# Attention scores of two heads at once on the two halves of TensorE's rows, in an attention, memory and mixture-of-experts layer

## The chip, the cores and the metric

The kernel runs on 1 core of one Trainium2 chip. The metric is the device time of one execution in microseconds (us). An execution is one launch that takes all inputs from the chip's main memory and leaves the output there.

## The reference, cut to what matters

The layer has an attention part and a part with 8 experts, each with a residual and a layer norm behind it. x has 8 batches of 512 positions and 256 features; there are 16 heads of 16 features. In the attention part a memory runs beside the softmax (decaying sums of outer products of 6-vectors), whose score gates a second value.

```python
B, T, D = x.shape                      # 8, 512, 256
H = decay_logits.shape[0]; dh = D // H # 16 heads of 16
qkv = (x @ qkv_w.T + qkv_b).reshape(B, T, 3, H, dh)
scores = jnp.einsum('bhtd,bhsd->bhts', q, k) * dh ** -0.5
scores = jnp.where(causal, -jnp.inf, scores)
attn = jax.nn.softmax(scores, axis=-1)
seq_out = jnp.einsum('bhts,bhsd->bhtd', attn, v)
...                                    # memory: lines, norms, decayed cumulative sums, gated
return (seq_out + gated * mem_val) @ out_w.T + out_b
# then: x = layernorm(x + attention); top-2 of 10 gates, 8 experts of 256 x 256; x = layernorm(x + ffn)
```

## The kernel before, in words

The program has three parts. The opening (about 0 to 95 us) computes the memory's projections of all batches, folds two weight matrices into one, and projects batch 0. The middle (about 78 to 545 us) is the attention of batch 0 to 7, with the memory's elementwise work on POOL beside it. Phase 3 (to the end) is the output projection, the layer norms and the experts; its weights are loaded and split beside the last batch.

The middle is made of groups: 4 heads of one batch, so 4 groups a batch, 32 in all. A group has 12 units (`UNITS`). Units 0 to 3 are the four heads' first tile of the triangle (512 columns), 4 to 7 the second (384), 8 and 9 the third (256, two heads each), 10 and 11 the last (128, padded to 256, two heads each). Scores are needed twice. `pe_max_scores` computes them with queries on the partitions, and DVE takes each row's maximum with the causal mask (`dve_max`, line 468, written to nmax); this runs 8 units (`LEAD`) ahead. `pe_exp_scores` computes them again with keys on the partitions, less the maximum, and ACT takes the exponential (`act_exp`, line 411) into Pr. POOL zeroes the upper triangle of the diagonal tiles (`pool_mask`, line 612). `pe_values` (line 338) multiplies Pr with V, in four strips of 17 of the array's columns, one strip a head, during the following group.

Numbers that must be more exact than one pass of the array gives are split in a high and a rest part. For that, Q and K stand in SBUF as stacks: three parts of 16 rows (high, high, rest against high, rest, high), 48 rows of zeros up to row 96 (`STACK`), and in rows 96 and 97 minus one in K against the high and rest part of the row maximum in Q. So a score matmul uses 96 or 98 of the array's 128 rows, and holds one head.

Each group also carries two of the 8 projections of the next batch (`pe_project`, line 374, six matmuls, at units 4 and 10), into one PSUM bank, J_ps. For j = 0 to 3 (Q and K) ACT copies the high part to HL (`act_project`, line 419), DVE the rest (`dve_project`, line 477), and SP writes HL to the main memory (`sp_projected`, line 623), from where `sp_stack` reads the stacks of a group in six DMAs. There is one HL, so the copy of j + 1 waits until the write of j has landed. For j = 4 to 7 ACT copies MV (line 422) and DVE adds to Vn (line 481). The input x of the next batch is split in xhi (ACT, line 438) and xlo (DVE, line 510) at unit 0 of the batch before, ahead of the first projection.

At unit 4 the maxima of the next group are transposed on TensorE (`pe_turn_max`, line 358), copied by DVE in a high and a rest part (`dve_turned_max`, lines 490 and 492), and written by SP with two DMAs to rows 96 and 97 of Q (`sp_max_rows`, line 643); the next group's first exponentials wait for them. At unit 7 ACT copies the values' bank O_ps to Osb (`act_out`), at unit 10 TensorE transposes it (`pe_turn_out`, line 351), and DVE divides by the sums (`dve_normalise`, lines 500 and 503). Both transposes use one bank, ps[5].

The order of all this is written out by hand: `pe_batch`, `act_batch`, `dve_batch`, `sp_batch` list for each engine what it does at which unit, and every engine works through its list in order. `need` waits for a semaphore. DVE's list also holds 36 scans of the memory (line 516), at units 6, 8, 10 or 0, 2, 4 of two groups in three from batch 2 on; POOL's list holds the masks between the memory's steps (lines 801 to 854). PSUM's 8 banks: three for the maxima's scores (S_ps), two for the exponentials' (ST_ps), one each for O_ps, the transposes, and J_ps.

## Time and profile before

| | us |
|---|---|
| median of 3 runs | 828.99 |
| lowest and highest run | 825.13, 829.65 |
| the profiled execution | 834.11 |
| its span, first to last instruction | 832.4 |
| TensorE busy in it | 734.4 (88%) |
| VectorE busy in it | 603.8 (73%) |
| ScalarE busy in it | 351.0 (42%) |
| GpSimd busy in it | 422.3 (51%) |

Engines are named as in the profile: PE is TensorE's matmuls, PEld its weight loads, DVE is VectorE, ACT ScalarE, POOL GpSimd, SP SyncE, which only issues DMAs here. Matmuls are pipelined and their ends are modelled, so PE's busy time holds more than its work; the distance from the start of one matmul to the start of the next is what it really takes in a dense stretch. PEclk is the clock that TensorE was granted, 1.00 being 2.4 GHz and 0.50 being 1.2 GHz. "Idle before, releaser" names what ended a wait.

### The profile page before, as it was taken

The page shows a single profiled execution, that of the slowest core. Times are in us where ns is not written, and L with a number is a line of the kernel's source. Part 1 is how long each engine was busy: PE and PEld are TensorE (multiplying, and loading weights), DVE is VectorE, ACT ScalarE, POOL GpSimd, SP SyncE. Part 2 cuts the span into 40 slices and gives each one's busy share as a digit, 9 for nine tenths or more (in the row PEclk, how much of TensorE's full clock was granted, in tenths as well). Part 3 has the DMA queues.
Part 4 walks back from the last instruction along what each step waited for, and adds up shares of the span by engine and source line. Part 5 has one row for each costly group of instructions (what it writes and reads, how often), then busy time and mean ns, then how long its engine had stood idle before and what let it go on. Part 6 is the DMA issues. An engine that isn't in the chain of part 4 may idle for free.

```text
span 832.4 us, 12395 instructions
## 1 busy us (share of the span) xinstructions
PE 734.4 (88%) x4004; PEld 495.0 (59%) x4004; DVE 603.8 (73%) x2105; ACT 351.0 (42%) x701; POOL 422.3 (51%) x334
## 2 busy tenths in 40 slices
PE   6993998898898998999898998878899899998995
PEld 3452655565565666565565664446677676776774
DVE  2344776778878888889688877736777877787785
ACT  2211555446454545555455555842242242232410
POOL 9200894996665676668476893424134042240410
PEclk9995999999998999999899997899999999999998
DMA  7899589675564574655734747220220302303000
GB/s 274 257 234 165 127 142 144 163 115 104 130 102 84 133 119 100 152 85 138 139 69 105 139 87 170 73 101 2 77 85 18 101 10 93 102 1 102 26 24 27
DMA packets 60420, 89.88 MB, mean 108 GB/s; under 512 B 8234, under 2 KB 37316, under 8 KB 60356
## 3 DMA queue, kind: packets, MB, share of 16 engines
q1 hardware_dynamic: 60356, 89.09, 47.7%
q8 instruction: 32, 0.52, 0.3%
q14 instruction: 32, 0.26, 0.1%
HBM read 54.72 MB, written 33.82 MB: 106 GB/s over the span
## 4 chain that ended last, share of the span: by engine, by line
PE 47%; DVE 23%; DMA 10%; POOL 9%; ACT 4%; issue 4%; SPq 2%; ACTq 0%; POOLq 0%; DVEq 0%
PE ps L1256 15%; PE ps L374 8%; PE ps L338 7%; PE ps L327 6%; PE ps L315 6%; DVE ps L468 5%; DMA Wm<-mem_scratch 3%; DVE Ob L516 3%; DMA Q<-MT 3%; DVE A L1390 3%; ACT X L1242 2%; PE ps L1221 2%; PE ps L232 1%; POOL Pr L612 1%; DVE Z L1276 1%
## 5 line engine op out<-in xcount | busy, mean ns | idle before, releaser
L468 DVE CUSTOM_DVE_ANT_0 ps<-ps,mask 128x256 f32<-128x256 f32 (+3 forms) x512 | 236.9, 509 | 31.8 <-PE ps L315 31.0
L411 ACT ACTIVATE Pr<-ps 128x512 f32<-128x512 f32 (+2 forms) x384 | 190.1, 528 | 114.8 <-PE ps L327 110.6
L327 PE MATMUL ps<-Q,K 98*128 98x256 f32 (+2 forms) x512 | 173.2, 380 | 28.9 <-DMA Q<-MT 21.9
L315 PE MATMUL ps<-K,Q 96*128 96x256 f32 (+2 forms) x512 | 157.9, 355 | 23.2 <-DVE nmax L468 22.5
L1256 PE MATMUL ps<-ew_hi,XT 128*128 128x512 f32 x512 | 176.2, 403 | 0.0
L1390 DVE SCALAR_TENSOR_TENSOR A<-ps,cw,A 128x256 f32<-128x256 f32 x256 | 123.6, 483 | 48.5 <-PE ps L1256 36.0
L327 PEld LDWEIGHTS ps<-Q,K 98*128 98x128 f32 x512 | 94.1, 197 | 104.8 <-ACT Pr L411 61.0
L612 POOL TENSOR_SCALAR_AFFINE_SELECT Pr<-Pr 128x512 f32<-128x512 f32 x128 | 88.3, 704 | 103.2 <-ACT Pr L411 100.8
L315 PEld LDWEIGHTS ps<-K,Q 96*128 96x128 f32 x512 | 103.0, 203 | 45.8 <-DVE nmax L468 28.3
L1256 PEld LDWEIGHTS ps<-ew_hi,XT 128*128 128x128 f32 x512 | 97.0, 189 | 21.2 <-issue 0.3
L1256 PE MATMUL ps<-ew_rest,XT 128*128 128x512 f32 x256 | 101.2, 395 | 0.0
L338 PE MATMUL ps<-Pr,V 128*17 128x512 f32 (+3 forms) x1024 | 99.9, 465 | 0.8 <-POOL Pr L612 0.8
L1194 POOL TENSOR_TENSOR A<-A,X 128x512 f32<-128x512 f32 x16 | 20.6, 1286 | 148.1 <-ACT A L1248 148.1
L468 DVE DVE_READ_ACCUMULATOR2_ANT nmax<- 128x1 f32 x512 | 69.5, 136 | 0.0
L419 ACT ACTIVATE HL<-ps,qkb 128x512 fp32r<-128x512 f32 x32 | 22.0, 687 | 81.9 <-PE ps L374 57.5
L1256 PEld LDWEIGHTS ps<-ew_rest,XT 128*128 128x128 f32 x256 | 48.6, 190 | 8.6
L374 PE MATMUL ps<-xhi,wqk 128*128 128x512 f32 x128 | 46.8, 450 | 3.5 <-DVE xlo L510 1.9
L852 POOL TENSOR_TENSOR Ob<-Ob,Rl 128x1533 f32<-128x1533 f32 x12 | 34.8, 2903 | 27.6 <-DVE Ob L516 27.6
L801 POOL TENSOR_TENSOR Ob<-Wm 128x511 f32<-128x511 f32 (+1 forms) x12 | 14.2, 1186 | 67.7 <-DMA Wm<-mem_scratch 67.5
L516 DVE TENSOR_TENSOR_SCAN Ob<-sc,Ob 128x512 f32<-128x512 f32 x36 | 45.7, 1269 | 0.0
L854 POOL TENSOR_TENSOR Wm<-Wm,Ob 128x1533 f32<-128x1533 f32 x12 | 43.4, 3613 | 0.9
L374 PE MATMUL ps<-wvc,xhi 128*128 128x512 f32 x128 | 42.8, 415 | 0.4 <-DVE bc L945 0.4
(190 smaller groups left out, 1049.2 us busy)
## 6 DMA issues: line engine op xcount, KB each, us to landing
qk_scratch<-HL SPq DMA_DIRECT2D x32, 512.0 KB, 3.2
Q<-qk_scratch SPq DMA_DIRECT2D x96, 128.0 KB, 4.4
K<-qk_scratch SPq DMA_DIRECT2D x96, 128.0 KB, 5.7
Pr<-xT SPq DMA_DIRECT2D x8, 512.0 KB, 7.0
xraw<-xT SPq DMA_DIRECT2D x8, 512.0 KB, 6.4
mem_scratch<-Rl SPq DMA_DIRECT2D x16, 256.0 KB, 7.5
mv_scratch<-MV SPq DMA_DIRECT2D x32, 128.0 KB, 1.8
Wm<-mem_scratch SPq DMA_DIRECT2D x16, 256.0 KB, 9.3
```

What stands on the lines that cost most here:

```text
L315: last = nc.tensor.matmul(o, Q[0:STACK, hh, P * i:P * i + P], K[0:STACK, hh, 0:n], start=True, stop=True)
L327: last = nc.tensor.matmul(o, K[0:STACK + 2, hh, P * kt:P * kt + P], Q[0:STACK + 2, hh, T - n:T], start=True, stop=True)
L338: last = nc.tensor.matmul(O_ps[32 * h:32 * h + VW, P * kt:T], V[:, kt, GROUP * g + h, :], probs(g % 2, kt, h, 1)[:, 0, :], start=(kt == 0) ...
L374: last = nc.tensor.matmul(J_ps[:], lhs, rhs, start=first, stop=(j < 4 and k == KT - 1 and a == 1))
L411: nc.scalar.activation(probs(g % 2, kt, heads[0], len(heads)), src, ACT.Exp, scale=SCALE).then_inc(s_exp, 1)
L468: last = nc.vector.tensor_tensor_reduce(out=scores, in0=scores, in1=mask[:, T - w:T], scale=1.0, scalar=NEG, op0=ALU.add, op1=ALU.max, acc ...
L516: nc.vector.tensor_tensor_scan(Ob[:, j % 3, :], col(SC_D).to_broadcast([P, T]), Ob[:, j % 3, :], 0.0, ALU.mult, ALU.add).then_inc(s_scan, 1)
L612: nc.gpsimd.affine_select(out=diagonal, in_=diagonal, compare_op=ALU.is_ge, fill=0.0, base=0, pattern=[[0, GROUP], [1, P]], channel_multip ...
L852: step(nc.gpsimd.tensor_tensor(Ob[:, :, 0:T - 1], Ob[:, :, 0:T - 1], Rl[:, i:i + 1, 1:T].to_broadcast([P, 3, T - 1]), ALU.mult))
L854: step(nc.gpsimd.tensor_tensor(Wm[:, lo:lo + 3, 0:T - 1], Wm[:, lo:lo + 3, 0:T - 1], Ob[:, :, 0:T - 1], ALU.add))
L1256: last = nc.tensor.matmul(o, lhs(c, k), rhs(d, k), start=first, stop=(k == KT - 1 and c == 1))
L1390: ins = nc.vector.scalar_tensor_tensor(acc, F_ps[v % 4][:, D * c:D * c + D], cw[:, par, i, e:e + 1], acc, ALU.mult, ALU.add)
```

## The change

- **Stacks.** `STACK` is 48: the three parts without zeros. Heads with an even number in the group have their stack in rows 0 to 47 (maxima in 48 and 49), odd ones in rows 64 to 111 (112 and 113), `HALF` being 64. Q and K are half as long (H // 2), and POOL's memsets of them at the start are two of 32 rows instead of three.
- **Scores in pairs.** `pe_max_scores` and `pe_exp_scores` are called for units u and u + 1 together and issue one matmul for a lower and one for an upper half, into two banks. S_ps has four banks, ST_ps two; the exponentials' pair waits until both have been read. Units 8 and 9, 10 and 11 hold heads 0 and 2, 1 and 3.
- **Banks.** The transposed output goes back to O_ps, the transposed maxima to J_ps, with waits for both.
- **HL, xhi and xlo twice.** HL alternates with j; its parts are written to memory by a DMA each, when each is ready. x is split a batch earlier, at units 10 and 11 of the last group.
- **Order.** Projections on PE at units 0 and 8 (was 4 and 10), their copies on ACT at 1 and 9 (4 and 10) and on DVE at 3 and 11 (5 and 11). The transposed output at unit 8 ahead of the projection (10, behind it), its division at 9 (10). The maxima are still transposed at unit 4, with no projection ahead of them; DVE copies them at 5 (4).
- **DMAs.** Eight for a group's stacks (six), four for the maxima's rows (two), two for HL (one).

```diff
-STACK = 96
+STACK = 48
+HALF = 64
-        S_ps, ST_ps = ps[0:2] + ps[7:8], ps[2:4]
-        O_ps, OT_ps, J_ps = ps[4:7]
-        M_ps = OT_ps
+        S_ps, ST_ps = [ps[0], ps[1], ps[7], ps[5]], ps[2:4]
+        O_ps, J_ps = ps[4], ps[6]
+        OT_ps, M_ps = O_ps, J_ps
...
+        def stacked(t, hh, n):
+            return t[HALF * (hh % 2):HALF * (hh % 2) + n, hh // 2, :]
...
         def pe_exp_scores(pe, b, g, u):
-            need(pe, s_exp, PU, b, UNITS * g + u - 1)
-            for c, h in enumerate(heads):
-                hh = GROUP * g + h
-                o = ST_ps[u % 2][:, c * 256:c * 256 + n]
-                last = nc.tensor.matmul(o, K[0:STACK + 2, hh, P * kt:P * kt + P], Q[0:STACK + 2, hh, T - n:T],
-                                        start=True, stop=True)
-            last.then_inc(s_st, 1)
+            need(pe, s_exp, PU, b, UNITS * g + u)
+            for c in range(len(unit_parts(u)[1])):
+                for v in (u, u + 1):
+                    kt, heads = unit_parts(v)
+                    hh = GROUP * g + heads[c]
+                    n = max(T - P * kt, 2 * P)
+                    ins = nc.tensor.matmul(ST_ps[v % 2][:, c * 256:c * 256 + n],
+                                           stacked(K, hh, STACK + 2)[:, P * kt:P * kt + P],
+                                           stacked(Q, hh, STACK + 2)[:, T - n:T], start=True, stop=True)
+                    if c == len(heads) - 1:
+                        ins.then_inc(s_st, 1)
...
         def pe_turn_out(pe, b, g):
             need(pe, s_oc, NG, b, g + 1)
-            need(pe, s_on, NG, b, g)
...
-        def pe_turn_max(pe, b, g):
+        def pe_turn_max(pe, b, g, projected):
             need(pe, s_max, PU, b, UNITS * (g + 1))
             need(pe, s_mt, 2 * NG, b, 2 * g)
-            need(pe, s_on, NG, b, g - 2)
+            pe.wait_ge(s_lo, projected)
...
-                for u in range(UNITS):
+                for u in range(0, UNITS, 2):
                     pe_exp_scores(pe, b, g, u)
...
-                    if u in (0, 2, 4, 6) and not (first and g == 0):
+                    if u < 8 and not (first and g == 0):
                         pe_values(pe, pb, pg, u // 2)
-                    if u in (4, 10) and not last:
-                        pe_project(pe, b + 1, 2 * g + u // 10)
+                    if u == 8 and not (first and g == 0):
+                        pe_turn_out(pe, pb, pg)
+                    if u in (0, 8) and not last:
+                        pe_project(pe, b + 1, 2 * g + u // 8, NG * b + g + 1 + u // 8)
                     if u == UNITS - LEAD and not (last and g == NG - 1):
-                        pe_turn_max(pe, b + (g + 1) // NG, (g + 1) % NG)
-                    if u == 10 and not (first and g == 0):
-                        pe_turn_out(pe, pb, pg)
+                        pe_turn_max(pe, b + (g + 1) // NG, (g + 1) % NG, min(8 * (b + 1) + 2 * g + 1, 8 * NB))
...
-                    if g == 0 and u == 0 and not last:
-                        act_split_x(act, b + 1)
-                    if u in (4, 10) and not last:
-                        act_project(act, b + 1, 2 * g + u // 10)
+                    if u in (1, 9) and not last:
+                        act_project(act, b + 1, 2 * g + u // 9)
+                    if (g, u) == (NG - 1, 10) and b < NB - 2:
+                        act_split_x(act, b + 2)
...
-                    if g == 0 and u == 0 and not last:
-                        dve_split_x(dve, b + 1)
-                    if u in (5, 11) and not last:
+                    if u in (3, 11) and not last:
                         dve_project(dve, b + 1, 2 * g + u // 11)
-                    if u == UNITS - LEAD and not (last and g == NG - 1):
+                    if u == UNITS - LEAD + 1 and not (last and g == NG - 1):
                         dve_turned_max(dve, b + (g + 1) // NG, (g + 1) % NG)
-                    if u == 10 and not (first and g == 0):
+                    if u == 9 and not (first and g == 0):
                         dve_normalise(dve, pb, pg)
...
             for r in range(2):
-                sp.dma_start(Q[STACK + r:STACK + r + 1, GROUP * g:GROUP * g + GROUP, :].rearrange(
-                    "o h (i t) -> o (h i) t", i=QT).bitcast(F32), MT[:, g % 2, r, :].bitcast(F32)).then_inc(s_mrow[g], 16)
+                for a in range(2):
+                    row = HALF * a + STACK + r
+                    sp.dma_start(Q[row:row + 1, 2 * g:2 * g + 2, :].rearrange("o c (i t) -> o (c i) t", i=QT).bitcast(F32),
+                                 MT[2 * QT * a:2 * QT * a + 2 * QT, g % 2, r, :].bitcast(F32)).then_inc(s_mrow[g], 16)
```

## Rows read from the trace of the kernel before

**Rows 1.** The page: busy us (share of the span) xinstructions.
```profile
PE 734.4 (88%) x4004; PEld 495.0 (59%) x4004; DVE 603.8 (73%) x2105; ACT 351.0 (42%) x701; POOL 422.3 (51%) x334
```

**Rows 2.** Stretches: us, busy per engine, PEclk, DMA share, GB/s.
```profile
130.00:187.40 57.40, 51.35 (x306) 32.58 (x306) 39.84 (x157) 27.28 (x55) 44.66 (x38) 0.94 0.78 140
187.40:486.70 299.30, 273.48 (x1642) 174.58 (x1641) 245.98 (x866) 154.28 (x311) 199.57 (x127) 0.95 0.57 114
486.70:545.00 58.30, 51.46 (x320) 30.45 (x318) 42.39 (x149) 37.46 (x76) 30.15 (x26) 0.85 0.39 102
473.70:486.70 13.00, 12.70 (x85) 8.41 (x85) 9.50 (x42) 7.00 (x16) 11.33 (x7) 1.00 0.77 107
```

**Rows 3.** Timeline of PE, one group: start, us, line, out<-in, columns, count.
```profile
477.30 0.63 PE L374 MATMUL ps<-wvc,xhi 128*128 128x512 f32 x2
...
478.69 0.28 PE L378 MATMUL ps<-bc,pick 96*128 96x256 f32 x1
...
479.17 0.48 PE L327 MATMUL ps<-Q,K 98*128 98x256 f32 x2
479.48 0.34 PE L315 MATMUL ps<-K,Q 96*128 96x384 f32 x1
479.66 0.40 PE L327 MATMUL ps<-Q,K 98*128 98x512 f32 x1
...
480.22 1.05 PE L338 MATMUL ps<-Pr,V 128*17 128x512 f32 x8
...
481.54 0.41 PE L315 MATMUL ps<-K,Q 96*128 96x256 f32 x2
481.78 0.40 PE L327 MATMUL ps<-Q,K 98*128 98x512 f32 x1
482.02 0.40 PE L315 MATMUL ps<-K,Q 96*128 96x256 f32 x2
482.35 0.84 PE L338 MATMUL ps<-Pr,V 128*17 128x384 f32 x8
483.11 0.50 PE L327 MATMUL ps<-Q,K 98*128 98x512 f32 x1
```

**Rows 4.** Waits from 95 to 545 us: total us, times, longest.
```profile
DVE MT L490 <- PE ps L358: 37.6, 26, 3.2
...
DVE rec L500 <- PE ps L351: 27.2, 22, 2.4
...
ACT HL L419 <- DMA qk_scratch<-HL: 16.2, 5, 4.1
...
POOL Ob L801 <- DMA Wm<-mem_scratch: 8.8, 1, 8.8
```

**Rows 5.** Timelines of DVE and PE at a batch's head, and stretches there.
```profile
258.71 2.63 DVE L510 TENSOR_TENSOR xlo<-xraw,xhi 128x1024 fp32r<-128x1024 f32 x1
...
262.27 0.77 PE L315 MATMUL ps<-K,Q 96*128 96x512 f32 x1 [2.31 <-DVE nmax L468]
...
259.00:263.00 4.00, 1.69 (x13) 0.94 (x13) 4.00 (x13) 0.98 (x2) 3.92 (x2) 0.80 0.95 107
263.00:266.00 3.00, 3.00 (x14) 1.78 (x14) 0.87 (x4) 0.00 (x0) 2.26 (x2) 0.50 0.36 142
```

**Rows 6.** Timeline of ACT: two exponentials and the wait before them.
```profile
483.65 0.98 ACT L411 ACTIVATE Pr<-ps 128x512 f32<-128x512 f32 x2 [0.83 <-PE ps L327]
...
481.74 1.09 ACT L411 ACTIVATE Pr<-ps 128x512 f32<-128x512 f32 x2 [0.99 <-PE ps L327]
```

**Rows 7.** SP's issue of the maxima's rows, and all their landings (line 643).
```profile
487.36 1.14 SPq L643 DMA_DIRECT2D Q<-MT  x2
...
DMA to landing us min/median/max: 1.8/2.7/11.4
```

**Rows 8.** The chain in the opening: start, us, what.
```profile
15.72 2.62 DMA qk_scratch<-HL
...
18.43 0.69 ACT HL L419
19.15 0.76 DVE HL L477
19.93 2.62 DMA qk_scratch<-HL
```

156 lines of the change are left out of this document (88 added, 68 removed).

## The prediction

> **What bounds the kernel now.** I read the page's busy times first, then one row per stretch for the middle of the kernel, then one undisturbed group on TensorE matmul by matmul, then the waits. The profiled execution took 834.11 us, 832.4 of it span. TensorE (PE) has the largest share, VectorE (DVE) the next [rows 1]. The middle of the kernel repeats one unit of work, a "group" (4 heads of one batch). From 187.4 to 486.7 us there are 20 of them, so 299.3 / 20 = 14.97 us each, in which DVE is busy 246.0 / 20 = 12.3 and POOL 10.0; an undisturbed group takes 13.0 with PE busy 12.7 [rows 2]. So PE sets the pace of the good groups, DVE stands close behind, and 2 us a group are lost on top.
>
> PE's 13.0 us in an undisturbed group, from where each matmul starts [rows 3]: a 512-column score matmul holds PE 0.24 us (481.78 to 482.02), a 384 one 0.18, a 256 one 0.12. A group has 16 scores for the maxima and 16 for the exponentials, each 4 x 0.24 + 4 x 0.18 + 8 x 0.12 = 2.6, together 5.2. Two projections are 2 x 1.39 (477.30 to 478.69), bias and transposes 0.48 and 0.2. The values (L338) take 1.05 and 0.84 us for 512 and 384 columns. That is 0.21 per 128 columns for all 8 matmuls of a call; a score streams 128 columns in 0.06 (0.24 / 4), so eight in turn would take 0.48 or more. The strips of 17 columns do run side by side. They stream 0.86 + 0.65 + 0.43 + 0.22 = 2.15. Round them stands a toll: the last score before them is over at 482.02 + 0.24 = 482.26, they start at 482.35, stream until 483.00, and the next score matmul loads at 483.11 and runs 0.1 later. So it costs 0.1 to go into another shape of the array and 0.2 to come out, 1.2 in four blocks. Sum: 5.2 + 2.8 + 0.7 + 2.15 + 1.2 = 12.05, so about 1 us of the 13.0 is waiting.
>
> The lost 2 us: ACT waits for the write of HL to land (16.2 us in five waits), DVE waits for the transposed maxima (37.6) and for the transposed output (27.2) [rows 4]. The worst place is at the head of a batch: the split of x on DVE takes 2.63 us, PE waits 2.31 for maxima behind it, the granted clock falls from full (2.4 GHz) to half (1.2 GHz), and the next matmuls take twice as long [rows 5].
>
> **The change part by part.**
> *Scores in pairs.* If the two halves run side by side as the column strips do, 16 pairs cost what 16 single ones cost: 2.6 instead of 5.2, so -2.6 us a group. The trace has no row halves; the bounds are 0 (they don't overlap) and -2.6. Between them: the strips of the values load only 17 columns of weights, the pairs 128 each, and a transpose, as short as the load allows, takes 0.11 to 0.12. Were two loads to follow each other, each of 16 pairs would cost at least 0.22, in all 3.5: -1.7. I take -2.6, nearest to the only rows with several tiles at once.
> The Trainium skill, "TensorEngine Tiling (Array Packing)", Key Properties, says that different tiles can load weights and multiply in parallel; it backs the value taken. The same section says that changing the tiling mode drains the engine, which speaks against this change; the trace agrees (0.1 in, 0.2 out).
> *Changes of shape.* Scores are now a third shape. The extra changes are projection to scores at unit 0, the transposed maxima at unit 4, and in and out of the full array at unit 8: four more, 0.2 each, +0.8. PE's own work is then 12.05 - 2.6 + 0.8 = 10.3.
> *Both ST banks at once.* A pair of exponentials' scores now waits until both banks are read. Turn-round: 0.4 for the matmuls, then two reads on ACT at 0.98 to 1.09 [rows 6], 1.4 to 1.5 us. Units 0, 4 and 8 give PE more own work than that between two pairs; at 2 and 6 it is about even; after unit 10 it is not: the projection's copy (0.4 to 0.7) and two reads stand before PE's next pair, against 0.4 of own work. I put 1.0 to 1.6 of waiting a group, so 11.3 to 11.9 for the loop of PE and ACT.
> *The maxima's rows.* DVE copies them at its unit 5, 7.3 us after the group's start in this order of work. SP then issues four DMAs instead of two, at 0.57 each (1.14 for two), and one lands after 1.8 to 2.7: 7.3 + 1.7 + 1.8 to 2.7 = 10.8 to 11.7 [rows 7]. This chain is as long as the loop: whenever DVE is late, the next group is late by as much. Behind them on SP's queue is only the next projection's write.
> *DVE.* Nothing is taken from it: 12.3 us a group remain from 187.4 on, more than PE and ACT want. It is the new bound. The waits for the transposes go, since PE now issues them before a projection and not behind it, and DVE reads a unit later. The split moves to the end of a batch with a second x: the same DVE time, but no projection waits for it. The second HL takes away the five waits for its landing. Eight stack DMAs for six add 0.9 us to SP, which is idle at that point; HL's write in two parts starts earlier.
> DVE's work is uneven (three scans of 1.2 us in two groups of three), so I don't expect 12.3 but about 1.1 more for meeting PE and ACT, as much as PE pays now in its best groups: 13.4. Saving: 20 x (14.97 - 13.4) = 31 us. With no loss it would be 53.
> *Before 187.4.* The first projections follow each other every 4.2 us because HL must land (2.6) first [rows 8]; without that, PE 1.6, ACT 0.7 and DVE 0.76 make 3.1. Three times 1.1 is 3 us; it can be lost again in the full DMA queues behind (0 to 5). The shorter memset on POOL hides behind these. Then POOL sets the pace: it is busy 44.7 of 57.4 us in 130 to 187.4 [rows 2] and waits 8.8 for its rows [rows 4], with masks between its long steps. I give this stretch 5 us (1 to 9).
> *The last batch and after.* No projections, the scores of the exponentials alone in pairs, clock 0.85 [rows 2]: 2 us (-1 to 4). Phase 3 is untouched: 0.
> Sum: 31 + 3 + 5 + 2 = 41. 834.1 - 41 = 793.1 for a profiled execution. Those of before have a median of 828.99, 5.1 lower: 788.
>
> **The rivals.**
> A. The weights of the two halves load one after the other, or the row chain or ACT's handshake costs a microsecond more than above. PE then stands at 11.2 plus waits, or the groups at 14.2. For it: 128 columns of weights each, and a chain with no slack. Against: the strips. 20 x 0.8 = 16 less is saved: 804.
> B. The halves don't overlap at all (both write PSUM at once, or nothing makes them tiles). PE's own work is 12.05 + 0.8 = 12.9, with ACT's wait 14.2 and DVE's unevenness about 15.0, as now. What is left is 3 + 5 and some of the landing waits: 824. Against: the strips of the values do overlap.
> C. Slower: the clock. PE's own work falls from 12.05 of 14.97 (80%) to 10.3 of 13.4 (77%), and its waiting gathers at the group's end (1 us, with DVE late 3). The trace shows the fall after a wait of 2.31 us, 3 us at half speed and more [rows 5]. A microsecond at half speed costs 0.5 x 0.77 = 0.39. The 41 us are gone when each of 28 groups spends 41 / 28 / 0.39 = 3.8 us more at half speed: a granted clock of about 0.80 in the middle instead of 0.95 [rows 2]. With one such fall of 5.5 us in each group: 788 + 28 x 5.5 x 0.39 = 848. Against: falls today follow waits of over 2 us, and the change removes the two commonest.
>
> **How the numbers follow.** Forecast 0.57, A 0.24, B 0.07, C 0.12. The forecast's ends: 20 x (14.97 - 12.3) + 5 + 9 + 4 = 71 saved gives 758; 14.0 a group and nothing elsewhere gives 810. The range runs from 758 to 832, over A and B and into the mild end of C; about 0.05 lies below and 0.12 above. A measurement here tells about 0.5% (4 us) from no change. B lies on both sides of that line and C's mildest cases are within it: faster 0.82, same 0.06, slower 0.12.
>
> **What would show it.** Right: the two scores of a pair start within some 10 ns; the 32 scores of a group take PE under 3 us; no wait of ACT for HL's landing in the middle; DVE's waits for the two transposes are small; the middle has 13 to 14 us a group with DVE busy over 90%. Wrong: starts of a pair 0.11 apart (A) or a whole matmul apart (B); a granted clock under 0.85 from 187 us on (C); PE waiting for the maxima's rows in most groups (A's row chain).

## The result and the profile after

| | before | after |
|---|---|---|
| median, us (4 runs each) | 829.32 | 854.99 |
| lowest and highest | 825.13, 831.29 | 849.70, 855.83 |
| span of the profiled execution | 832.4 | 853.6 |
| mean granted clock in it | 0.946 | 0.891 |

The ratio is 1.0303, 95% interval 1.0245 to 1.0361: 3% slower, where 788 us, 5% faster, had been predicted, and outside the range of 758 to 832. It was measured beside new runs of the kernel before. Here and below a ratio is formed from undisturbed executions alone, so it is not exactly the quotient of the medians beside it.

The page of the changed kernel first: busy times (they answer rows 1), the granted clock in 40 slices, and the two groups of score matmuls.

```profile
span 853.6 us, 12579 instructions
...
PE 690.4 (81%) x4004; PEld 425.8 (50%) x4004; DVE 602.5 (71%) x2105; ACT 349.0 (41%) x701; POOL 409.1 (48%) x333
...
PEclk9996888989696899898797798587999999999998
...
L490 DVE CUSTOM_DVE_ANT_0 ps<-ps,mask 128x256 f32<-128x256 f32 (+3 forms) x512 | 237.7, 512 | 118.9 <-PE ps L331 118.7
...
L346 PE MATMUL ps<-Q,K 50*128 50x256 f32 (+2 forms) x512 | 102.2, 437 | 91.6 <-DMA Q<-MT 50.5
...
L331 PE MATMUL ps<-K,Q 48*128 48x256 f32 (+2 forms) x512 | 81.1, 356 | 11.1 <-DVE nmax L490 8.7
```

The same two kinds of line on the page of the kernel before:

```profile
PEclk9995999999998999999899997899999999999998
...
L327 PE MATMUL ps<-Q,K 98*128 98x256 f32 (+2 forms) x512 | 173.2, 380 | 28.9 <-DMA Q<-MT 21.9
```

TensorE is busy 690 us instead of 734 and yet the kernel is longer. The scores of the exponentials (L346, was L327) took 173 us and take 102, but idle time in front of them is 92 us, mostly for the maxima's rows (Q<-MT). The slices of the clock tell of a second thing: behind the opening seven slices stand at 5 to 7 tenths, where the kernel before has one.

The stretches of rows 2, by the same limits:

```profile
core 0: us, PE busy (x) PEld busy (x) DVE busy (x) ACT busy (x) POOL busy (x), PEclk, DMA share, GB/s
130.00:187.40 57.40, 41.85 (x291) 22.60 (x284) 39.05 (x150) 27.42 (x57) 42.42 (x35) 0.85 0.68 143
187.40:486.70 299.30, 236.53 (x1572) 125.18 (x1573) 237.98 (x835) 146.66 (x297) 194.54 (x126) 0.86 0.41 111
486.70:545.00 58.30, 44.21 (x318) 21.79 (x318) 41.31 (x173) 32.82 (x68) 30.18 (x24) 0.82 0.47 134
```

In the middle PE is busy 236.5 us of 299.3 (273.5 before), DVE 238.0 (246.0), at a clock of 0.86 (0.95). No engine is busier than 80%: DVE, which was to be the new bound, has become idler.

The pair itself does what was hoped. The timeline of TensorE, against rows 3:

```profile
start us, us, engine line op out<-in xcount [idle before <-releaser]
305.60 0.28 PE L374 MATMUL ps<-ident,nmax 128*16 128x128 f32 x1
305.83 0.44 PE L346 MATMUL ps<-Q,K 50*128 50x384 f32 x2
306.11 0.39 PE L331 MATMUL ps<-K,Q 48*128 48x512 f32 x2
306.43 0.41 PE L359 MATMUL ps<-Pr,V 128*17 128x128 f32 x8
```

Two matmuls of 384 columns (x2) are over after 0.28 us and two of 512 after 0.32; one by one they take 0.18 and 0.24 each. The second of a pair starts with the first, not behind it: the trace has the two of 384 columns 4 ns apart and the two of 512 columns 1 ns, and over the whole run no pair for the exponentials is further apart than 9 ns and none for the maxima than 39. The 0.1 above the streaming is the toll of changing the array's shape, once in front of the block (0.28 - 0.18) and once behind it (0.32 - 0.24), of the size of the toll round the values before. Part 3 of the Trainium skill's page "TensorE: Matmul & The Clock Gate" says that matmuls on different row groups run concurrently and start some 4 ns apart; the trace agrees (1 and 4 ns here).

The waits from 95 to 545 us, against rows 4:

```profile
engine line waited for: us in total, times, longest us
DVE ps L490 <- PE ps L331: 103.8, 79, 4.9
...
ACT Pr L429 <- PE ps L346: 98.6, 92, 6.2
...
PEld ps L346 <- DMA Q<-MT: 55.7, 23, 6.3
PEld ps L346 <- ACT Pr L429: 53.4, 69, 2.0
PE ps L346 <- DMA Q<-MT: 41.4, 12, 6.0
PE ps L346 <- ACT Pr L429: 35.8, 71, 2.5
...
PEld ps L391 <- DVE xlo L534: 14.0, 5, 5.5
...
PEld ps L391 <- DVE HL L499: 11.1, 8, 3.3
PE ps L391 <- DVE xlo L534: 9.1, 3, 4.5
```

Two lines of the same view of the kernel before, for comparison:

```profile
DVE ps L468 <- PE ps L315: 19.2, 26, 2.6
...
PE ps L327 <- DMA Q<-MT: 11.5, 9, 2.2
```

DVE's waits for the two transposes (37.6 and 27.2) and ACT's for HL's landing (16.2) are gone from this list, as forecast. In their place DVE waits 103.8 us for scores of the maxima (19.2 before), and TensorE 41.4 for the maxima's rows (11.5) and 35.8 for ACT (6.0).

How a group comes to wait for its rows is seen on SyncE's queue (SPq, its issuing of DMAs). The second block has the other engines in the same stretch: TensorE at the start of the group, DVE's second copy of the transposed maxima, TensorE at the start of the next group:

```profile
156.34 0.60 SPq L649 DMA_DIRECT2D qk_scratch<-HL  x1
...
160.71 3.15 SPq L667 DMA_DIRECT2D Q<-qk_scratch  x4
163.91 1.82 SPq L667 DMA_DIRECT2D K<-qk_scratch  x4
165.77 1.52 SPq L649 DMA_DIRECT2D qk_scratch<-HL  x2
167.34 3.29 SPq L676 DMA_DIRECT2D Q<-MT  x4
```
```profile
154.76 0.49 PE L346 MATMUL ps<-Q,K 50*128 50x512 f32 x2 [1.37 <-DMA Q<-MT]
...
163.02 0.28 DVE L515 TENSOR_TENSOR MT<-ps,MT 16x128 fp32r<-16x128 f32 x1
...
172.52 0.80 PE L346 MATMUL ps<-Q,K 50*128 50x512 f32 x2 [6.01 <-DMA Q<-MT]
...
173.67 1.91 PE L359 MATMUL ps<-Pr,V 128*17 128x512 f32 x8
```

A write of HL is given out at 156.34. Next in the list are the stacks, which read that write and so wait for its landing: their first issue is at 160.71, 4.4 us after the write was given out. Eight issues of stacks then take 5.0 us, two of the next HL 1.5, and the four of the maxima's rows begin at 167.34. The rows had been ready since 163.02 + 0.28 = 163.3. They take 3.3 us to give out (0.6 to 1.2 each), and TensorE goes on at 172.52 after a wait of 6.0, at half clock: its values (L359) take 1.91 us where rows 3 show 1.05. From one group's start to the next it is 17.8 us: 8.5 until the rows are copied, 4.0 in which they wait for the queue, 3.3 to give them out, 1.9 until TensorE goes on.

### The profile page after: what moved, and what is told of

Same layout as the page of the kernel before. It is cut to its first block, busy times and chain, and to the rows that moved or that the text cites. A ratio compares the mean times of both kernels' runs of the same rounds, so it can differ in the third digit from the quotient of the medians.

```text
span 853.6 us, 12579 instructions
## 1 busy us (share of the span) xinstructions
PE 690.4 (81%) x4004; PEld 425.8 (50%) x4004; DVE 602.5 (71%) x2105; ACT 349.0 (41%) x701; POOL 409.1 (48%) x333
## 4 chain that ended last, share of the span: by engine, by line
PE 43%; DVE 22%; DMA 10%; SPq 10%; ACT 8%; issue 5%; POOL 2%; ACTq 0%; DVEq 0%; POOLq 0%
PE ps L1289 15%; PE ps L391 9%; PE ps L346 6%; PE ps L359 5%; DVE ps L490 5%; DMA Q<-MT 4%; ACT Pr L429 4%; DMA qk_scratch<-HL 4%; SPq L667 3%; DVE Ob L540 3%; SPq L676 3%; DVE A L1423 3%; PE ps L331 2%; PE ps L1254 2%; PE ps L238 2%
## 5 line engine op out<-in xcount | busy, mean ns | idle before, releaser
L429 ACT ACTIVATE Pr<-ps 128x512 f32<-128x512 f32 (+2 forms) x384 | 183.0, 523 | 129.2 <-PE ps L346 124.5
L346 PE MATMUL ps<-Q,K 50*128 50x256 f32 (+2 forms) x512 | 102.2, 437 | 91.6 <-DMA Q<-MT 50.5
L346 PEld LDWEIGHTS ps<-Q,K 50*128 50x128 f32 x512 | 47.9, 202 | 165.9 <-DMA Q<-MT 65.2
L359 PE MATMUL ps<-Pr,V 128*17 128x512 f32 (+3 forms) x1024 | 109.3, 505 | 1.5 <-DVE On L526 0.7
L1289 PEld LDWEIGHTS ps<-ew_hi,XT 128*128 128x128 f32 x512 | 97.2, 190 | 21.2 <-issue 0.3
L331 PE MATMUL ps<-K,Q 48*128 48x256 f32 (+2 forms) x512 | 81.1, 356 | 11.1 <-DVE nmax L490 8.7
L391 PE MATMUL ps<-xhi,wqk 128*128 128x512 f32 x128 | 53.2, 504 | 14.6 <-DVE xlo L534 11.2
L331 PEld LDWEIGHTS ps<-K,Q 48*128 48x128 f32 x512 | 55.4, 212 | 18.6 <-DVE nmax L490 12.1
L391 PE MATMUL ps<-wvc,xhi 128*128 128x512 f32 x128 | 48.4, 462 | 1.8 <-DVE Vn L504 1.3
L391 PEld LDWEIGHTS ps<-xhi,wqk 128*128 128x128 f32 x128 | 27.5, 238 | 36.7 <-DVE xlo L534 14.0
```

The source lines that it names most:

```text
L331: ins = nc.tensor.matmul(S_ps[v % 4][:, c * 256:c * 256 + n], stacked(Q, hh, STACK)[:, P * i:P * i + P], stacked(K, hh, STACK)[:, 0:n], st ...
L346: ins = nc.tensor.matmul(ST_ps[v % 2][:, c * 256:c * 256 + n], stacked(K, hh, STACK + 2)[:, P * kt:P * kt + P], stacked(Q, hh, STACK + 2)[ ...
L359: last = nc.tensor.matmul(O_ps[32 * h:32 * h + VW, P * kt:T], V[:, kt, GROUP * g + h, :], probs(g % 2, kt, h, 1)[:, 0, :], start=(kt == 0) ...
L391: last = nc.tensor.matmul(J_ps[:], lhs, rhs, start=first, stop=(j < 4 and k == KT - 1 and a == 1))
L429: nc.scalar.activation(unit_probs(g % 2, kt, heads), src, ACT.Exp, scale=SCALE).then_inc(s_exp, 1)
L1289: last = nc.tensor.matmul(o, lhs(c, k), rhs(d, k), start=first, stop=(k == KT - 1 and c == 1))
```

## The experiments

Each run was timed beside new executions of the kernel before on the same chip. "Mean clock" and "half clock" are of one profiled execution each. "Half clock" is the time that TensorE spent at 1.2 GHz between 95 and 490 us of it: twice (1 - PEclk) times 395 us, from the clock before rounding. Before it is 37.5 us, after 112.6. The 37.5 is on the high side: the profiled execution of the kernel before has a clock of 0.946, and the executions of it timed beside the runs below have 0.949 to 0.953 in the mean of each batch of runs. The expectations name theories by letters, each explained where it first stands.

| run | median us | ratio, 95% interval | mean clock | half clock |
|---|---|---|---|---|
| after | 854.99 | 1.0303 (1.0245 to 1.0361) | 0.891 | 112.6 |
| rows_first | 841.67 | 1.0172 (1.0088 to 1.0256) | 0.901 | 85.2 |
| x_early | 852.22 | 1.0320 (1.0237 to 1.0404) | 0.893 | 98.5 |
| rows_first_x_early | 844.50 | 1.0182 (1.0108 to 1.0257) | 0.897 | 92.2 |
| before_more_dmas | 831.27 | 1.0025 (0.9984 to 1.0067) | 0.949 | 34.1 |
| r_two_waits | 840.44 | 1.0123 (1.0086 to 1.0161) | 0.896 | 92.2 |
| r_unpaired | 849.08 | 1.0141 (1.0050 to 1.0232) | 0.885 | 121.4 |
| r_twice | 864.14 | 1.0403 (1.0346 to 1.0460) | 0.943 | 30.7 |
| r_old_order | 883.80 | 1.0609 (1.0528 to 1.0691) | 0.871 | 132.6 |
| r_old_order_98_rows | 851.18 | 1.0260 (1.0183 to 1.0338) | 0.945 | 37.5 |
| before_half_rows | 916.71 | 1.1046 (1.0918 to 1.1173) | 0.839 | 156.1 |
| before_stack_late | 853.12 | 1.0293 (1.0214 to 1.0371) | 0.937 | 51.2 |
| r_64_rows | 843.53 | 1.0151 (1.0075 to 1.0228) | 0.906 | 78.6 |
| r_unpaired_98_rows | 839.21 | 1.0161 (1.0071 to 1.0252) | 0.946 | 47.8 |
| r_filler | 851.32 | 1.0310 (1.0216 to 1.0404) | 0.931 | 31.2 |
| old_order_early_98_rows | 862.99 | 1.0426 (1.0335 to 1.0517) | 0.938 | 51.2 |
| before_128_rows | 825.04 | 0.9959 (0.9916 to 1.0002) | 0.962 | 20.5 |
| before_128_rows_32_columns | 825.24 | 0.9927 (0.9893 to 0.9960) | 0.960 | 20.5 |
| r_64_rows_32_columns | 839.97 | 1.0115 (1.0076 to 1.0154) | 0.910 | 78.2 |

### SyncE's queue, the split of x, the number of transfers

rows_first puts the reads of the stacks behind the rows of the maxima in `sp_batch`:

```diff
-                if g == 0 and not first:
-                    sp_stack(sp, b, NG - 1)
-                if g and not last:
-                    sp_stack(sp, b + 1, g - 1)
                 if not (last and g == NG - 1):
                     sp_max_rows(sp, b + (g + 1) // NG, (g + 1) % NG)
+                if g == 0 and not first:
+                    sp_stack(sp, b, NG - 1)
+                if g and not last:
+                    sp_stack(sp, b + 1, g - 1)
```

> The changed kernel with one edit: in each group SP issues the eight stack DMAs behind the maxima's rows instead of ahead of HL's write and the rows. Theory S (SP's queue holds the rows back; PE then waits 4 to 6 us and its clock falls): PE's wait for the rows (50.5 us in the changed kernel) falls below 15, TensorE's time at half clock between 95 and 490 us falls from 113 to under 70 us, the kernel takes 805 to 825 us. Theory C (the array in halves, or its lower load, keeps the clock down by itself): the wait for the rows falls but half clock stays over 100 us, 840 to 855 us. Theory O (the new order of projections and copies sets the pace): the wait falls, the time stays within 1.5% of the changed kernel, over 842 us.

x_early splits x one group sooner, since the changed kernel has its split at units 10 and 11 of a batch's last group and its first use at unit 0 of the next:

```diff
-                    if (g, u) == (NG - 1, 10) and b < NB - 2:
+                    if (g, u) == (NG - 2, 10) and b < NB - 2:
                         act_split_x(act, b + 2)
```

> The changed kernel with the split of x one group earlier (units 10 and 11 of the third group instead of the fourth). Theory X (the split stands right ahead of the projection that needs it, behind DVE's scans): the waits of PE for xlo (11.2 us) vanish and the time falls by 1 to 1.5% (two to three batches of seven lose 5 us and a fall of the clock each), to 842 to 847 us. If DVE's queue as a whole is late and not the split, the wait only moves to the next name and the time stays within 0.5% of 855.

rows_first_x_early is both.

> Both edits. If S and X are separate losses, their gains add: 795 to 815 us, under the kernel before (829). If they are one chain with two names, it is no better than the better of the two by over 0.5%.

before_more_dmas is the kernel before with 8, 4 and 2 transfers instead of 6, 2 and 1:

```diff
-                sp.dma_start(qk_scratch[b, j], HL[:].bitcast(F32)).then_inc(s_scr[j // 2], 16)
+                for s, done in ((0, s_hi), (1, s_lo)):
+                    need(sp, done, 8, b, j + 1, apart=True)
+                    sp.dma_start(qk_scratch[b, j, :, s], HL[:, s].bitcast(F32)).then_inc(s_scr[j // 2], 16)
...
+                for a in range(2):
+                    h0 = GROUP * g + 2 * a
```

> The kernel before with only the DMA counts of the change: eight for a group's stacks (was six), four for the maxima's rows (two), two for HL (one), all bytes and the order kept. Theory S: SP needs 2.5 to 3.5 us more a group ahead of the rows' landing; with a single HL and groups of 15 us it shows in part, 838 to 855 us. If the DMA count is not what matters, 829 within 0.5%.

In rows_first the wait that stood in the changed kernel's list shrinks:

```profile
DVE ps L490 <- PE ps L331: 82.7, 71, 4.4
...
PE ps L346 <- ACT Pr L429: 44.0, 80, 4.7
...
PE ps L346 <- DMA Q<-MT: 16.3, 8, 5.0
```

TensorE's wait for the rows falls from 41.4 to 16.3 us, the median by 13.3 (the ratios by 1.3%, 11 us, with intervals that just overlap; the profiled spans are 853.6 and 838.4). The same move on top of x_early took 7.7 us off the median (852.22 to 844.50), again with intervals that just overlap. SyncE's wait for a landing of HL in front of the stacks, 27.1 us in seven waits from 95 to 490, is no longer there. So this queue is some 8 to 13 of the 26 us lost, a third to a half. None of the three theories of rows_first was met whole: the wait fell as theory S said, but half clock stayed at 85.2 us, not under 70, and the time at 842, not 805 to 825. x_early removes the waits for xlo and gains nothing; the number of transfers alone costs nothing in the old order. Both theories behind those two runs fell, and the two edits together are no better than the first alone.

### The handshake, the pairing, the order

The next four start from rows_first. r_two_waits lets each half of a pair of exponentials' scores wait for its own bank:

```diff
-            need(pe, s_exp, PU, b, UNITS * g + u)
+            need(pe, s_exp, PU, b, UNITS * g + u - 1)
...
+                    if c == 0 and v == u + 1:
+                        need(pe, s_exp, PU, b, UNITS * g + u)
```

> The base is the run rows_first (841.67 us, 1.0172 of before). One change: the first half of a pair of scores for the exps waits for its own bank's exp, the second half for the other's, where the changed kernel waits for both before either. Theory H (the handshake on the two ST banks is what the rest of the loss consists of): PE L346 waits 44.0 us for ACT in 95 to 545; at least half of it goes and the time falls by 10 us or more, to under 832. Theory C (TensorE does less work per microsecond, its granted clock stays at 1.2 GHz longer, and what the halves save is paid back): the first half of the pair starts earlier but the second still waits for its bank and the two no longer lie beside each other, so the time is within 4 us of the base, 838 to 846, and time at half clock between 95 and 490 stays at 75 to 95 us. Theory O (the new order of the projections and the shared PSUM banks cost the rest): the same as C, no gain over 4 us.

r_unpaired issues the scores one by one, from half the rows:

```diff
-                    pe_exp_scores(pe, b, g, u)
-                    on, ng, nu = ahead(g, u)
-                    if not (last and on):
-                        pe_max_scores(pe, b + on, ng, nu)
+                    for v in (u, u + 1):
+                        pe_one_exp(pe, b, g, v)
+                        on, ng, nv = ahead(g, v)
+                        if not (last and on):
+                            pe_one_max(pe, b + on, ng, nv)
```

> The base is rows_first. One change: the scores are issued one unit at a time again (exp u, maxima of u, exp u+1, maxima of u+1), still from half the rows each; banks, order of the projections, transfers and layout stay as in the changed kernel. TensorE's score time goes back from about 184 to about 330 us. Theory C: the engine does more per microsecond, the granted clock holds, time at half clock between 95 and 490 falls from 85 us to 50 or less, and the total is no slower than the base, 828 to 843, although 140 us of TensorE time came back. Theory H: the ACT wait of L346 (44.0 us) goes to under 15, and the total is 828 to 838. Theory O: the order and the banks stay, so their cost stays, and the score time comes on top: 846 to 870.

r_twice issues every pair twice (`for q in range(2 * nh): c = q % nh`).

> The base is rows_first. Every matmul pair of scores is issued twice into the same place (its output is unchanged), so TensorE's score work is that of the kernel before while the handshake, the banks and the order stay those of the changed kernel. If the halved score work were a gain that is merely hidden under other losses (theories H and O), taking it away costs: each pair holds its bank some 0.24 to 0.5 us longer, 880 to 930 us. Theory C: the added work keeps the granted clock up, time at half clock between 95 and 490 falls from 85 to under 50 us, and the total is within 12 us of the base, 832 to 854.

r_old_order is r_unpaired with the list of work and the banks of the kernel before (`S_ps[v % 3]`, `OT_ps = ps[5]`, `M_ps = OT_ps`, the old `pe_batch`).

> The base is rows_first. Its layout, transfers, double HL and double split of x stay; scores one unit at a time from half the rows, and the order and the banks of the kernel before (three banks for the maxima's scores, a bank of its own for the two transposes, projections at units 4 and 10, maxima turned at unit 4). Against r_unpaired it differs by order and banks alone. Theory O: 820 to 832, and r_unpaired at least 12 us slower than this. Theory C and H: this and r_unpaired within 8 us of each other, both 826 to 838. If the layout or the transfers cost something in themselves, this run is the one that shows it: over 836.

r_two_waits lies inside the interval of rows_first (1.0123 against 1.0172): TensorE's waits for ACT at L346 fell from 44.0 to 10.6 us (its line there is L348), and the time by 4 us, if anything. But in about half of its pairs the two now start up to 1.1 us apart, and PE's busy time from 95 to 490 rose from 320.6 to 343.7 us, so this run takes back part of the pairing and doesn't price the handshake alone. r_unpaired adds TensorE time on half the rows: half clock rose to 121.4 us where theory C had asked for 50 or less, and the time is that of theory O (846 to 870, 849.08 measured). r_twice issues every pair twice and loses 2.3% to rows_first, between what theory C (within 12 us) and the others (5 to 10%) had asked for; its clock is the best of these four (0.943). More of the same work on the same rows does raise the clock. r_old_order was the surprise. The old order, far from bringing the old time back, gave 884 us, with TensorE's slices of the clock down to 0.5:

```profile
span 882.1 us, 12562 instructions
...
PE 769.5 (87%) x4004; PEld 487.6 (55%) x4004; DVE 607.4 (69%) x2105; ACT 352.2 (40%) x701; POOL 408.6 (46%) x333
...
PEclk9996688689878878889897888567999999999998
```

TensorE is busy 770 us of 882 with the same matmuls and the same columns as before (734 of 832), only each on 48 or 50 rows instead of 96 or 98. No theory that I had then said this, and theory K was made from it: the clock follows the rows in use.

### The rows in use

before_half_rows takes the kernel before and cuts the contraction alone:

```diff
-                last = nc.tensor.matmul(o, Q[0:STACK, hh, P * i:P * i + P], K[0:STACK, hh, 0:n], start=True, stop=True)
+                last = nc.tensor.matmul(o, Q[0:48, hh, P * i:P * i + P], K[0:48, hh, 0:n], start=True, stop=True)
...
-                last = nc.tensor.matmul(o, K[0:STACK + 2, hh, P * kt:P * kt + P], Q[0:STACK + 2, hh, T - n:T],
+                last = nc.tensor.matmul(o, K[0:50, hh, P * kt:P * kt + P], Q[0:50, hh, T - n:T],
```

> The kernel before with one change: the matmuls of the maxima contract over rows 0 to 47 instead of 0 to 95, those of the exps over rows 0 to 49 instead of 0 to 97; so the third part of the sum and the maxima are left out of what is computed. Nothing else differs: the same instructions, columns, transfers, order. Theory K (what holds TensorE's clock up counts the rows in use, so half the rows let it fall although the engine is as long busy): the clock falls between 95 and 545, mean granted clock under 0.91 (before 0.95), half clock between 95 and 490 at 75 us or more (37.5 before), total 850 to 885. Theory O/L (in the run of the old order, 883.8 us, the layout and the transfers cost the time): no change here, 826 to 834, clock 0.94 to 0.96.

r_old_order_98_rows goes the other way, `Q[0:BROWS, hh // 2, ...]` and `K[0:BROWS + 2, hh // 2, ...]` (96 and 98 rows) in the run of the old order. Like every run below that widens the rows in the changed layout, it also zeroes two more strips of 32 rows of Q at the start.

> The base is r_old_order (883.8 us, clock 0.871). One change: the matmuls of the scores contract over rows 0 to 95 and 0 to 97, so each sums two heads' products (its output is not the reference's); order, banks, columns, transfers and layout stay. Theory K: the clock comes back to 0.94 or more and the time to 820 to 840. Theory L (layout and transfers): 870 to 890 as in the base.

r_64_rows widens the pairs of the exponentials, with zeros in Q:

```diff
-                                           stacked(K, hh, STACK + 2)[:, P * kt:P * kt + P],
-                                           stacked(Q, hh, STACK + 2)[:, T - n:T], start=True, stop=True)
+                                           stacked(K, hh, HALF)[:, P * kt:P * kt + P],
+                                           stacked(Q, hh, HALF)[:, T - n:T], start=True, stop=True)
```

> The base is rows_first (841.67 us, clock 0.901, 85.2 us at half clock between 95 and 490). One change: the pairs of the exps contract over all 64 rows of their half, of which the last 14 are zeros in Q, so a pair uses 128 rows instead of 100 and computes the same. Theory K, if rows that hold zeros count: half clock between 95 and 490 falls to 60 to 80 us, total 830 to 840. If only the columns or the values count: within 3 us of the base.

before_stack_late moves the same lines as rows_first, in the kernel before.

> The kernel before with one change: on SyncE's queue the reads of the stacks stand behind the two row transfers of the maxima, as in rows_first. Asked: is the queue's order worth anything by itself in the kernel before, whose waits of L338 for the maxima's rows are small? Theory S says little, 824 to 832; below 824 it would be the fastest kernel here.

The twenty groups of the middle, first of the kernel before with half the rows, then of the kernel before with 128 rows (below). Before, these groups took 299.3 us with PE busy 273.5 at 0.95 [rows 2].

```profile
212.40:553.60 341.20, 326.20 (x1642) 201.59 (x1641) 250.19 (x865) 156.38 (x310) 201.09 (x127) 0.80 0.50 100
```
```profile
183.00:477.90 294.90, 267.75 (x1642) 171.92 (x1641) 245.37 (x865) 153.83 (x311) 201.32 (x128) 0.97 0.58 116
```

The instructions, columns and order are the same in half the rows, and the kernel takes 917 us instead of 829, more than theory K's 850 to 885; the middle groups take 341.2 us at a clock of 0.80. The values that flow differ too, since the maxima are left out. In the old order the rows are worth 33 us: 883.8 and 851.2, clock 0.871 and 0.945; the clock is back, the time is not within theory K's 820 to 840. That it is the rows and not the values in them rests on several runs together: r_old_order computes the right values on half the rows and has the low clock, the kernel before computes them on 96 and 98 and has the high one, and both runs of 98 rows in the changed layout, where each score sums two heads, have the high one as well. A run with the same rows and other values was not made. r_64_rows, which adds 28 rows to half of the pairs, moved neither time nor clock beyond their spread (its four runs were granted 0.899 to 0.907, those of rows_first 0.894 to 0.905), where theory K had 830 to 840 us for rows that hold zeros. The page "TensorE: Matmul & The Clock Gate" of the Trainium skill, Part 1, says that the gate follows how busy TensorE has been; these runs show that busy time alone doesn't tell it.

before_stack_late shows that rows_first is no rule: the same move makes the old order 2.9% slower, since there the scores of the maxima wait for the stacks (K<-qk_scratch, 16.7 us from 95 to 545, 0.4 in the whole kernel before). 824 to 832 had been expected.

### The clock in the changed order, and what beats both

r_unpaired_98_rows is r_unpaired over 96 and 98 rows.

> The base is r_unpaired (849.08 us median, 121.4 us at half clock between 95 and 490): the changed kernel's order, banks and transfers with the stacks behind the rows, scores one unit at a time. One change: the matmuls of the scores contract over 96 and 98 rows instead of 48 and 50, so each sums two heads' products (its output is not the reference's). Theory K (the clock follows the rows in use): half clock between 95 and 490 falls to under 60 us. If the clock is then all that separates the changed order from the kernel before, 822 to 834; if the order and the shared banks cost something beside it, 835 to 850.

r_filler adds full-row work where TensorE waits for the rows:

```diff
+            need(pe, s_exp, PU, b, UNITS * g + u)
             if u == 0:
+                if not (isinstance(b, int) and b == NB - 1):
+                    for _ in range(6):
+                        nc.tensor.matmul(ST_ps[0][:], wqk[0][:, 0, 0:P], wqk[0][:, 0, :], start=True, stop=True)
                 need(pe, s_mrow[g], 64, b, 64)
-            need(pe, s_exp, PU, b, UNITS * g + u)
```

> The base is rows_first (841.67 us; half clock between 95 and 490 85.2 us). Added: before each group's wait for the rows of its maxima, six matmuls of 128 rows and 512 columns of weights on weights, into a bank that the scores then overwrite (28 groups, 168 matmuls, at 0.24 to 0.48 us each 40 to 80 us of TensorE work; the output stays the same). Some of it lies under the waits for the rows (16.3 us on the matmuls and 35.6 on the loads in the base). Theory K: half clock falls to under 60 us and the total grows by far less than the work added, 832 to 852. If work on the path simply adds: 870 to 900.

before_128_rows:

```diff
-            for t in (Q, K):
-                nc.gpsimd.memset(t[0:STACK].bitcast(F32), 0.0).then_inc(s_cch, 1)
+            for t, n in ((Q, P), (K, STACK)):
+                nc.gpsimd.memset(t[0:n].bitcast(F32), 0.0).then_inc(s_cch, 1)
...
-            nc.gpsimd.memset(K[STACK:STACK + 2].bitcast(F32), -1.0).then_inc(s_cst, 1)
+            nc.gpsimd.memset(K[STACK:P].bitcast(F32), -1.0).then_inc(s_cst, 1)
...
-                last = nc.tensor.matmul(o, K[0:STACK + 2, hh, P * kt:P * kt + P], Q[0:STACK + 2, hh, T - n:T],
+                last = nc.tensor.matmul(o, K[:, hh, P * kt:P * kt + P], Q[:, hh, T - n:T],
```

> The kernel before with one change: the matmuls of the exps contract over all 128 rows instead of 98; the 30 added rows are zeros in Q, so the same is computed, with the same instructions and columns. Theory K, if rows of zeros count: half clock between 95 and 490 falls from 37.5 to 20 to 32 us and the total to 818 to 828. If they don't count, or what is left at half clock lies in waits: 826 to 832.

old_order_early_98_rows is r_old_order_98_rows with the stacks ahead again.

> The base is r_old_order_98_rows (851.18 us). One change: SyncE's queue gives out the stacks ahead of the projections' writes and the maxima's rows again, as in the kernel before. Against the kernel before there remain the layout on two halves, 8, 4 and 2 transfers instead of 6, 2 and 1, HL and the split of x held twice; each matmul sums two heads' products. If these cost nothing: 816 to 832, and below 826 if the two copies of HL save what ACT waits for its writes (16.2 us in 95 to 545 before). If they cost: over 836.

The last two add 15 columns to the values' loads (those of the next head, whose results are never read), to before_128_rows and to r_64_rows:

```diff
-                last = nc.tensor.matmul(O_ps[32 * h:32 * h + VW, P * kt:T], V[:, kt, GROUP * g + h, :],
+                v0 = VW * (H * kt + GROUP * g + h)
+                last = nc.tensor.matmul(O_ps[32 * h:32 * h + 32, P * kt:T], Vf[:, v0:v0 + 32],
```

> The base is before_128_rows (825.04 us, 0.9959 of before, 20.5 us at half clock between 95 and 490). One change: the matmuls of the values load 32 columns of V instead of 17 (the 15 more are those of the next head, their results are never read), so they use more of the array for the same time. If columns in use count for the clock as rows do: half clock between 95 and 490 under 12 us, total 816 to 824, faster than before beyond its interval. If not: 823 to 828.

> The base is r_64_rows (843.53 us, half clock 78.6 us between 95 and 490 and 44.4 between 490 and 600): the changed kernel with the stacks behind the rows and exps over 64 rows. One change: the values load 32 columns of V instead of 17. If columns in use count: half clock between 95 and 490 falls to 35 to 60 us and the total to 825 to 838. Should it come to under 829, the pairs are worth having once the clock holds. If columns don't count: 840 to 846.

Twenty middle groups of the three forms of the changed order with the stacks behind, each between the same two copies of the maxima: single scores on half the rows (r_unpaired), single scores on 98 rows (r_unpaired_98_rows), pairs (rows_first).

```profile
192.60:499.60 307.00, 275.86 (x1648) 155.00 (x1640) 243.66 (x865) 152.10 (x311) 205.34 (x128) 0.84 0.40 112
```
```profile
187.30:483.60 296.30, 266.27 (x1641) 172.41 (x1640) 244.00 (x865) 152.81 (x311) 206.37 (x128) 0.94 0.41 116
```
```profile
191.90:486.80 294.90, 235.98 (x1644) 126.86 (x1640) 243.94 (x866) 152.18 (x311) 202.45 (x129) 0.90 0.42 116
```

The lines stand in this order. Half the rows cost 10.7 us at the same number of columns (307.0 against 296.3, clock 0.84 against 0.94). Pairing gives 12.1 back (294.9, clock 0.90) and so ends where the full rows had been: PE's busy time falls from 266 to 236 us and the groups don't get shorter. These are single executions; the timed ratios of the three (1.0141, 1.0161, 1.0172) can't tell them apart, their clocks can (0.879 to 0.900, 0.943 to 0.946, 0.894 to 0.905 over all runs of each). r_filler adds 168 matmuls of 0.24 to 0.48 us and takes the half clock from 85.2 to 31.2 us, but the total grows by 10: what the clock gives back doesn't pay for the work put in.

The same 20 groups take 299.3 us in the kernel before. With the queue's order changed the middle of the paired kernel is thus 4.4 us shorter than before, and what rows_first still loses lies elsewhere. Its first copy of the transposed maxima comes at 68.2 us (63.7 before, 63.0 in before_more_dmas, whose profiled execution lies nearer to the median), the first eight groups take 2.7 us more than in before_more_dmas, the last three 4.0, and 1.7 are lost behind the last copy:

```profile
L515 DVE TENSOR_TENSOR MT<-ps,MT x32: 278/279/280, 68.2 to 532.6; 16x128 fp32r<-16x128 f32 x32
```

The layout is not free. old_order_early_98_rows has the old order, the old place of the stacks, the full rows and a clock of 0.938, and is 4.3% slower than before. SyncE waits 25.6 us for HL's landing in it from 95 to 490 (13.6 before), TensorE 26.1 for the maxima's rows from 95 to 545 (11.5). Since before_more_dmas has as many transfers and loses nothing, it is the second HL, the place of the split or the other shape of the transfers that does this; which of them was not tried. The traces show one such difference: a part of HL takes SyncE 0.60 us to give out in the changed layout and 0.33 in before_more_dmas, at the same 256 KB.

before_128_rows_32_columns has the lowest ratio here, 0.7% below before, interval 0.4% to 1.1%, but its median is that of before_128_rows (825.24 and 825.04), and the intervals of the two overlap. Its mean clock over 11 runs is 0.963, that of before_128_rows 0.959 (10 runs), that of the kernel before beside them 0.953 and 0.952. Half clock is 20.5 us in both, where under 12 had been asked for if columns count, so an effect of the columns is not shown. In the paired kernel the two steps came to 1.0115 against 1.0172, with intervals that overlap, and half clock stayed at 78 us (35 to 60 had been asked for).

## Why the prediction was wrong

**The pair.** Right. 16 pairs for 32 matmuls, fully side by side; rival A's loads in turn and rival B (no overlap) are out. The toll of the change of shape is 0.1 in front of a block and 0.1 behind it, the 0.2 that was put on each change.

**DVE's waits and HL.** Right: the waits of rows 4 for the transposes and for HL's landing went.

**The handshake of ACT.** Right in size: 1.0 to 1.6 us a group were put on it; TensorE waits 35.8 us for ACT in 95 to 545, some 30 groups, 1.2 each.

**The maxima's rows. The first step that failed.** The chain was priced at 7.3 + 1.7 + 1.8 to 2.7 = 10.8 to 11.7 us, with SyncE free when the copies are ready, and the text looked at what stands behind the rows on the queue, not at what stands ahead: the stacks, and with them the landing of an HL that in this order is written just before. In the group shown the rows are copied after 8.5 us instead of 7.3, then wait 167.34 - 163.30 = 4.0 us for the queue, where the sum has nothing, and the four issues take 3.3 us instead of 2.3 (four at 0.57): 17.8 us in all. Of the stack issues only the two added ones were costed, at 0.9 us "on SP, which is idle at that point"; it wasn't, and here all eight, 5.0 us, stand ahead of the rows. rows_first and rows_first_x_early price the place of the stacks at 8 to 13 us. The rival that named this chain (A's) had it a microsecond or so too long, for 804 us.

**The clock. The second.** Rival C named a mechanism that did come, and got 0.12; the central sum has the clock at no cost. Its argument against itself was that falls follow waits of over 2 us and that the change removes the two commonest. New waits came (the rows), and the rows in use, which it doesn't have, count as well: 917 us for half the rows, at unchanged columns and order. A pair uses as many rows as a single score did, but for half the time. Rival C asked for a clock of about 0.80 in the middle for all of the gain to go; 0.86 was measured, with new waits for the rest. Its price per microsecond at half speed was 0.39 us; over the whole span before_half_rows spent 203 us more there and took 77 us longer, 0.38 each, r_old_order 133 and 31 more than its 98-row form, 0.23, r_unpaired 105 and 16, 0.15. The changed kernel spent 97 us more at half clock than before, which by these is 15 to 37 us, as an estimate: a good part of the 41 that were to be gained. These prices are of other kernels, and time at half clock in which TensorE only waits costs nothing, so no run shows the figure.

**DVE as the new bound. The third.** The same 20 groups as in rows 2, counted between the same two copies of the maxima, took 310.7 us:

```profile
194.80:505.50 310.70, 246.75 (x1640) 131.29 (x1640) 244.92 (x865) 152.43 (x311) 199.63 (x127) 0.86 0.41 110
```

That is 15.5 us each, against 14.97 before and 13.4 forecast, with DVE busy 12.2 as before. TensorE's saved 2.6 us a group became waiting: in groups like the one shown the row chain ends last. With the chain shortened (rows_first) it is 14.7, a gain of 0.2 a group where 1.6 were put. The shortest group did fall from 11.4 to 10.2 us and the shortest with a projection from 12.5 to 11.6.

**The split of x.** "No projection waits for it" was wrong (9.1 us on matmuls, 14.0 on loads): it is a batch earlier in the list's index, but its use follows two units later. x_early shows that this cost nothing by itself; the wait moved.

**Opening and end.** 3 + 5 + 2 us of gain were forecast. The first copies of the transposed maxima are at 63.7 us before and 67.1 after, the last at 528.4 and 547.7, and 304.0 and 305.9 us follow it: of the 21.2 us between the two spans 3.4 are lost in the opening, 15.9 in the middle, 1.9 behind.

```profile
L515 DVE TENSOR_TENSOR MT<-ps,MT x32: 278/279/280, 67.1 to 547.7; 16x128 fp32r<-16x128 f32 x32
```
```profile
L492 DVE TENSOR_TENSOR MT<-ps,MT x32: 278/279/279, 63.7 to 528.4; 16x128 fp32r<-16x128 f32 x32
```

The opening shows where its 3 us went, after first and then before: the last read of K's first stack, and TensorE's first scores, which need it.

```profile
34.25 1.83 SPq L667 DMA_DIRECT2D K<-qk_scratch  x4
...
41.15 0.73 PE L331 MATMUL ps<-K,Q 48*128 48x512 f32 x4 [2.31 <-DMA K<-qk_scratch]
41.81 5.40 PE L238 MATMUL ps<-Pr 128*128 128x512 f32 x8
```
```profile
31.17 1.41 SPq L637 DMA_DIRECT2D K<-qk_scratch  x3
...
39.58 0.93 PE L315 MATMUL ps<-K,Q 96*128 96x512 f32 x3 [0.38 <-DMA K<-qk_scratch]
40.34 3.60 PE L232 MATMUL ps<-Pr 128*128 128x512 f32 x8
```

K's reads are given out 3.5 us later (36.1 instead of 32.6), TensorE waits 2.3 us instead of 0.4 and starts 1.6 later, and its clock is 0.5 from 42.5 to 45.9, where before it is 1.00: the next eight matmuls take 1.8 us more. All kernels of the changed layout wait there for 2.3 to 4.6 us, those of the old layout for 0.8 at most (0.5 in before_more_dmas, with as many transfers). The prediction counted the wait for HL's landing alone.

**What adds up and what stays open.** Of 26 us, 8 to 13 are SyncE's queue (rows_first, rows_first_x_early). About as much is left with single scores on full rows at the clock of before (r_unpaired_98_rows, 1.0161), so the rest doesn't need the pairs; the order, the banks and the layout are what the two have in common. The traces of rows_first and before_more_dmas put it in the opening (5.2 us), the first and last groups and the end, not in the 20 groups of the middle, and for all but the opening its cause stays open. old_order_early_98_rows shows that the layout can cost in the middle too (320.1 us for the 20 groups), but only in the old order with the stacks ahead, and its parts weren't separated. The pairs against r_unpaired_98_rows: 30 us less of TensorE in the middle, 1.4 us in time, with 37 us more at half clock. That the clock took all of the pairs' gain, and not the other waits of the group a part of it, is not shown: no run had pairs at a full clock without added work.

## What to carry to other kernels

Halving the time of matmuls where they are not the last thing waited for buys waiting, and here the clock fell with it; look first at what each group really ends on. Before moving or adding a transfer read its queue from the front: what is given out ahead of it, and on which landing that waits. And a matmul that has rows to spare can be widened over zeros: in the kernel before this cost nothing and came with a clock of 0.959 for 0.952 and a time 0.4% lower, which is hardly beyond the spread; in the paired kernel it did nothing.
